# A fused attention and expert layer: maxima, values and normalising placed anew on VectorE and ScalarE

## What is computed

```python
qkv = x @ qkv_w.T + qkv_b
scores = einsum('bhtd,bhsd->bhts', q, k) * scale        # causal: -inf above the diagonal
attn = softmax(scores, axis=-1)
seq_out = einsum('bhts,bhsd->bhtd', attn, v)
...                                                     # write and read lines, decayed outer products, cumulative sums
mem_val = x @ memv_w.T + memv_b
gated = mean(sigmoid(mem_score_t * mem_scale) * gate)
y = (seq_out + gated * mem_val) @ out_w.T + out_b
x = layernorm(x + y)
x = layernorm(x + experts(x))                           # top 2 of 10, 8 real experts
```

## Time and profile before

| what | us |
|---|---|
| median of 3 runs | 800.92 |
| lowest and highest | 799.39 and 806.83 |
| the profiled execution | 804.29 |
| its span in the profile | 802.6 |

### The profile page before, as it was taken

One profiled execution on the slowest core, in us unless ns is written; L12 is line 12 of the kernel. 1 busy time (PEld: TensorE's weight loads), 2 busy tenths in 40 slices (PEclk: granted clock), 3 DMA queues, 4 the chain that ended last, 5 costly groups with the idle time before them and its releaser, 6 DMA issues.

```text
span 802.6 us, 12373 instructions
## 1 busy us (share of the span) xinstructions
PE 715.8 (89%) x4004; PEld 500.0 (62%) x4004; DVE 604.7 (75%) x2105; ACT 351.0 (44%) x701; POOL 424.7 (53%) x334
## 2 busy tenths in 40 slices
PE   5998989998989998989999986879999999999995
PEld 2555665665656666666666754457767677676774
DVE  2257776879998889788898776547777778787785
ACT  2314555555545556465554566632224232242311
POOL 9300899995675757686776860612405134051310
PEclk9997998999999999999999996879999999999998
DMA  8786462524334334334325253032030330303000
GB/s 282 253 269 214 141 190 95 191 87 142 124 97 145 130 94 147 120 107 152 95 74 167 83 172 113 1 106 80 0 106 1 105 100 7 106 1 105 27 27 26
DMA packets 60084, 89.87 MB, mean 112 GB/s; under 512 B 7898, under 2 KB 36980, under 8 KB 60020
## 3 DMA queue, kind: packets, MB, share of 16 engines
q1 hardware_dynamic: 60020, 89.09, 34.0%
HBM read 54.72 MB, written 33.82 MB: 110 GB/s over the span
## 4 chain that ended last, share of the span: by engine, by line
PE 51%; DVE 29%; ACT 6%; issue 5%; POOL 4%; DMA 4%; SPq 1%; ACTq 0%; DVEq 0%; POOLq 0%
PE ps L1252 15%; PE ps L375 9%; DVE ps L470 7%; PE ps L339 7%; PE ps L328 7%; PE ps L316 6%; DVE Ob L518 4%; DVE A L1386 3%; PE ps L232 2%; PE ps L1217 2%; ACT X L1238 2%; ACT Pr L413 2%; DVE Z L1272 1%; DVE HL L479 1%; PE ps L352 1%
## 5 line engine op out<-in xcount | busy, mean ns | idle before, releaser
L470 DVE CUSTOM_DVE_ANT_0 ps<-ps,mask 128x256 f32<-128x256 f32 (+3 forms) x512 | 237.2, 510 | 20.9 <-PE ps L316 20.3
L413 ACT ACTIVATE Pr<-ps 128x512 f32<-128x512 f32 (+2 forms) x384 | 190.0, 529 | 117.1 <-PE ps L328 111.3
L328 PE MATMUL ps<-Q,K 98*128 98x256 f32 (+2 forms) x512 | 174.0, 382 | 12.7 <-ACT Pr L413 9.1
L316 PE MATMUL ps<-K,Q 96*128 96x256 f32 (+2 forms) x512 | 153.9, 346 | 28.5 <-DVE nmax L470 28.0
L1252 PE MATMUL ps<-ew_hi,XT 128*128 128x512 f32 x512 | 176.3, 403 | 0.0
L614 POOL TENSOR_SCALAR_AFFINE_SELECT Pr<-Pr 128x512 f32<-128x512 f32 x128 | 90.3, 721 | 141.4 <-ACT Pr L413 138.9
L1386 DVE SCALAR_TENSOR_TENSOR A<-ps,cw,A 128x256 f32<-128x256 f32 x256 | 123.6, 483 | 47.2 <-PE ps L1252 34.5
L328 PEld LDWEIGHTS ps<-Q,K 98*128 98x128 f32 x512 | 93.8, 197 | 64.5 <-ACT Pr L413 27.2
L316 PEld LDWEIGHTS ps<-K,Q 96*128 96x128 f32 x512 | 100.4, 199 | 48.8 <-DVE nmax L470 36.2
L1252 PEld LDWEIGHTS ps<-ew_hi,XT 128*128 128x128 f32 x512 | 97.1, 190 | 21.3 <-issue 0.3
L1252 PE MATMUL ps<-ew_rest,XT 128*128 128x512 f32 x256 | 101.4, 396 | 0.0
(11 more groups left out here) (190 smaller groups left out, 1044.6 us busy)
## 6 DMA issues: line engine op xcount, KB each, us to landing
qk_scratch<-HL SPq DMA_DIRECT2D x32, 512.0 KB, 2.7
Q<-qk_scratch SPq DMA_DIRECT2D x96, 128.0 KB, 2.8
K<-qk_scratch SPq DMA_DIRECT2D x96, 128.0 KB, 2.7
Pr<-xT SPq DMA_DIRECT2D x8, 512.0 KB, 5.6
xraw<-xT SPq DMA_DIRECT2D x8, 512.0 KB, 4.2
mem_scratch<-Rl SPq DMA_DIRECT2D x16, 256.0 KB, 4.0
mv_scratch<-MV SPq DMA_DIRECT2D x32, 128.0 KB, 1.7
Wm<-mem_scratch SPq DMA_DIRECT2D x2, 2048.0 KB, 9.7
```

The costliest lines, as they stand in the source:

```text
L316: last = nc.tensor.matmul(o, Q[0:STACK, hh, P * i:P * i + P], K[0:STACK, hh, 0:n], start=True, stop=True)
L328: last = nc.tensor.matmul(o, K[0:STACK + 2, hh, P * kt:P * kt + P], Q[0:STACK + 2, hh, T - n:T], start=True, stop=True)
L413: nc.scalar.activation(probs(g % 2, kt, heads[0], len(heads)), src, ACT.Exp, scale=SCALE).then_inc(s_exp, 1)
L470: last = nc.vector.tensor_tensor_reduce(out=scores, in0=scores, in1=mask[:, T - w:T], scale=1.0, scalar=NEG, op0=ALU.add, op1=ALU.max, acc ...
```

## The change

- The high copy of the turned maxima goes from VectorE to ScalarE (`act_turned_max`, at unit 4 behind the exponential and the projection's copies). VectorE's subtraction goes from unit 4 to unit 5, behind its maxima and projection step.
- `dve_normalise` goes from unit 10 to unit 11, again behind both, and multiplies in one operation of four dimensions.
- `V` becomes two buffers, by batch. ScalarE writes the values straight from the projection's bank, once for each of projections 4 to 7, behind `MV`. `Vn`, `act_values`, the semaphore `s_vc` and VectorE's bias add are gone.
- The value bias goes into `bc`, which gets 512 columns; the product with `pick` runs over the whole bank. `vb` moves into a part of `Pr`, and in `fold` ScalarE and VectorE each have one operation more for `bc`.
- The weights' loads of the last batch wait for the value products of the batch before (`s_pv`) in place of `s_vc`.

```diff
-        bc = sb("bc", [STACK, D], F32R)
+        bc = sb("bc", [STACK, 2 * D], F32R)
...
-        Vn = sb("Vn", [P, QT, D], F32, part2)
+        V = [sb("V0", [P, QT, H, VW], F32, part2)]
...
+        vb = Pr[:, 1, 3456:3456 + D]
...
             if kt == 0:
-                need(pe, s_vc, 1, b, 1)
+                need(pe, s_lo, 8, b, 8)
...
-                last = nc.tensor.matmul(J_ps[:, D:2 * D], pick[:], bc[:], start=False, stop=True)
+                last = nc.tensor.matmul(J_ps[:], pick[:], bc[:], start=False, stop=True)
...
                 nc.scalar.activation(MV[:, j % 2, :], J_ps[:, D:2 * D], ACT.Identity).then_inc(s_hi, 1)
 
+                need(act, s_pv, NG, b, -NG)
+                nc.scalar.activation(V[b % 2][:, j - 4, :, 0:DH], J_ps[:, 0:D].rearrange("p (h d) -> p h d", h=H),
+                                     ACT.Identity).then_inc(s_lo, 1)
...
-        def act_values(act, b):
-            need(act, s_lo, 8, b, 8)
-            need(act, s_pv, NG, b, 0)
-            nc.scalar.activation(V[:, :, :, 0:DH], Vn[:].rearrange("p i (h d) -> p i h d", h=H),
-                                 ACT.Identity).then_inc(s_vc, 1)
+        def act_turned_max(act, b, g):
+
+            need(act, s_mtr, NG, b, g + 1)
+            if g >= 2:
+                need(act, s_mrow[g - 2], 32, b, 32)
+            else:
+                need(act, s_mrow[g + 2], 32, b, 0)
+            nc.scalar.activation(MT[:, g % 2, 0, :], M_ps[0:GROUP * QT, 0:P], ACT.Identity).then_inc(s_mt, 1)
...
-                    if g == 0 and u == 8:
-                        act_values(act, b)
+                    if u == UNITS - LEAD and not (last and g == NG - 1):
+                        act_turned_max(act, b + (g + 1) // NG, (g + 1) % NG)
...
-            else:
-                need(dve, s_vc, 1, b, 0)
-                nc.vector.tensor_tensor(Vn[:, j - 4, :], J_ps[:, 0:D], vb[:], ALU.add).then_inc(s_lo, 1)
 
         def dve_turned_max(dve, b, g):
 
-            need(dve, s_mtr, NG, b, g + 1)
-            if g >= 2:
-                need(dve, s_mrow[g - 2], 32, b, 32)
-            else:
-                need(dve, s_mrow[g + 2], 32, b, 0)
-            nc.vector.tensor_copy(MT[:, g % 2, 0, :], M_ps[0:GROUP * QT, 0:P]).then_inc(s_mt, 1)
             need(dve, s_mt, 2 * NG, b, 2 * g + 1)
...
-            for i in range(QT):
-                last = nc.vector.tensor_tensor(
-                    On[:, i, GROUP * DH * g:GROUP * DH * (g + 1)].rearrange("p (h c) -> p h c", h=GROUP),
-                    turned[:, i, :, 0:DH], rec[:, i, :].unsqueeze(2).to_broadcast([P, GROUP, DH]), ALU.mult)
-            last.then_inc(s_on, 1)
+            nc.vector.tensor_tensor(
+                On[:, :, GROUP * DH * g:GROUP * DH * (g + 1)].rearrange("p i (h c) -> p i h c", h=GROUP),
+                turned[:, :, :, 0:DH], rec[:].unsqueeze(3).to_broadcast([P, QT, GROUP, DH]),
+                ALU.mult).then_inc(s_on, 1)
...
-                    if u in (5, 11) and not last:
+                    if u in (5, 11) and g < 2 and not last:
                         dve_project(dve, b + 1, 2 * g + u // 11)
-                    if u == UNITS - LEAD and not (last and g == NG - 1):
+                    if u == UNITS - LEAD + 1 and not (last and g == NG - 1):
                         dve_turned_max(dve, b + (g + 1) // NG, (g + 1) % NG)
-                    if u == 10 and not (first and g == 0):
+                    if u == 11 and not (first and g == 0):
                         dve_normalise(dve, pb, pg)
...
                     sp.wait_ge(s_lo, NB * 8)
-                    sp.wait_ge(s_vc, NB)
+                    sp.wait_ge(s_pv, NG * (NB - 1))
...
-                nc.scalar.activation(bc[:], OT_ps[0:STACK, 0:D], ACT.Identity).then_inc(s_wr, 1)
+                nc.scalar.activation(bc[:, D:2 * D], OT_ps[0:STACK, 0:D], ACT.Identity)
+                act.wait_ge(s_ws, 5 * 16)
+                nc.scalar.activation(bc[:, 0:D], vb[0:STACK], ACT.Identity).then_inc(s_wr, 1)
...
-                nc.vector.tensor_tensor(bc[32:64], OT_ps[32:64, 0:D], bc[32:64].bitcast(F32),
+                nc.vector.tensor_tensor(bc[32:64, D:2 * D], OT_ps[32:64, 0:D], bc[32:64, D:2 * D].bitcast(F32),
+                                        ALU.subtract)
+                dve.wait_ge(s_ws, 5 * 16)
+                nc.vector.tensor_tensor(bc[32:64, 0:D], vb[32:64], bc[32:64, 0:D].bitcast(F32),
                                         ALU.subtract).then_inc(s_wl, 1)
```

More of the change, by code:

```diff
@@ L114, in build @@
         Pr = sb("Pr", [P, 2, GROUP * T * 5 // 2], F32, part2)
-        V = sb("V", [P, QT, H, VW], F32, part2)
+        V.append(sb("V1", [P, QT, H, VW], F32, part2))
         Osb = sb("Osb", [P, T], F32, part2)
@@ L181, in build @@
         s_onst = sem("s_onst")
-        s_vc = sem("s_vc")
         s_mw = [sem(f"s_mw{i}") for i in range(3)]
@@ L335, in pe_values @@
             if kt == 0:
-                need(pe, s_vc, 1, b, 1)
+                need(pe, s_lo, 8, b, 8)
                 need(pe, s_oc, NG, b, g)
             for h in range(GROUP):
-                last = nc.tensor.matmul(O_ps[32 * h:32 * h + VW, P * kt:T], V[:, kt, GROUP * g + h, :],
+                last = nc.tensor.matmul(O_ps[32 * h:32 * h + VW, P * kt:T], V[b % 2][:, kt, GROUP * g + h, :],
                                         probs(g % 2, kt, h, 1)[:, 0, :], start=(kt == 0), stop=(kt == QT - 1))
@@ L688, in build @@
             expert_w=expert_w, expert_b=expert_b, out=out, mv_scratch=mv_scratch, o_scratch=o_scratch,
-            weights_space=3 * KT * T + 2 * T + QT * D + 2 * D + 8 * KT * D + 4 + D,
+            weights_space=3 * KT * T + 2 * T + QT * H * VW + 2 * D + 8 * KT * D + 4,
             s_onst=s_onst, s_gm=s_gm, s_max=s_max, max_count=NB * PU, s_oc=s_oc, s_on=s_on, outs=NB * NG))
@@ L716, in _ @@
                              (col(SC_GB), memg_b), (col(SC_MIX), iter_mix.to_broadcast([P, 1])),
-                             (vb[:], v_b.to_broadcast([P, D]))):
+                             (vb, v_b.to_broadcast([P, D]))):
                 sp.dma_start(dst, src).then_inc(s_ws, 16)
@@ L760, in _ @@
             nc.gpsimd.memset(pick[:].bitcast(F32), 0.0).then_inc(s_cch, 1)
-            nc.gpsimd.memset(V[:, :, :, DH:VW], 1.0)
+            for v in V:
+                nc.gpsimd.memset(v[:, :, :, DH:VW], 1.0)
             nc.gpsimd.iota(iota_i[:], pattern=[[1, NE]], base=0, channel_multiplier=0)
@@ L913, in _ @@
             act.wait_ge(s_wl, 4)
+            act_turned_max(act, 0, 0)
             act_batch(act, 0, first=True)
@@ L940, in fold @@
                 nc.vector.tensor_tensor(wvc[1][:], wst_vc, wvc[0][:].bitcast(F32), ALU.subtract).then_inc(s_wl, 1)
[L941 removed]
+                nc.vector.tensor_tensor(bc[32:64, D:2 * D], OT_ps[32:64, 0:D], bc[32:64, D:2 * D].bitcast(F32),
+                                        ALU.subtract)
+                dve.wait_ge(s_ws, 5 * 16)
+                nc.vector.tensor_tensor(bc[32:64, 0:D], vb[32:64], bc[32:64, 0:D].bitcast(F32),
                                         ALU.subtract).then_inc(s_wl, 1)
             def project(j):
[L945 to L947 removed]
+                if j < 4:
+                    dve_project(dve, 0, j)
             def scores(u0):
```

4 lines of the change are left out of this document (removed).

## The result

| | us |
|---|---|
| after, median of 4 executions (791.14 to 795.53) | 792.64 |
| before, median of 3 executions (799.39 to 806.83) | 800.92 |
| ratio, with its 95% interval | 0.988 (0.985 to 0.992) |
| the profiled execution of after | 792.37 |
| its span | 790.6 |

Executions of before more than 1.5% above its fastest (811.59 beside this result, four later ones) are counted as slow and left out of every number here. The change saves about one per cent: 8.3 us between these medians, and 8.4 to 9.1 against three later medians of before (801.0, 801.6 and 801.7 over 20, 18 and 14 executions).

A forecast was written before the change was run, and what follows sets the result against it. TensorE was taken to pace groups without scans and VectorE most groups with scans, where the excess could be won. Terms summed to -5.7, with clock -1.6 to -7.3: 793.5 us from the median of 800.92, range 786 to 800.5.

The forecast's parts named there:

- opening: Before the first value products: one more ScalarE copy and VectorE subtraction for bc, less a maxima copy, +0.4; longer bias products, +0.4.
- scans at 6, 8, 10: Six groups with scans at these units: scan and maxima start sooner, normalising falls under value products; 0.8 each, -4.8 us.
- scans at 0, 2, 4: Six groups with scans at these units: VectorE saves 0.31 each, 0.34 more in three with values; -2.3 us.
- reciprocals: Four groups: a 936 ns reciprocal behind the pair at unit 4 and the normalising at unit 10 fills the wait; -2.0 us.
- rows' DMA: Copies of turned maxima, units 4 and 5: waiting for the rows' DMA was the risk; the whole term was +0.1 us.
- bias +1.7: Bias product of 512 columns for 256: 0.11 us each, 16 times on TensorE's path in eight plain groups.
- clock -1.6: Two closing waits run into half-clock stretches of 3.4 us; with shorter waits one of the two stretches goes, -1.6 us.
- last batch: Normalising behind unit 11's maxima delays the store of On and the weights' loads behind it by 0.8; +0.8 us.
- closing wait: TensorE's wait for maxima before unit 2's value products, in groups with scans at 6, 8, 10: from 1.1 to about 0.3.
- the rival in which the clock holds: All five low-clock stretches between 178 and 437 us go, 8 us instead of 1.6: about 787; chance 0.18.
- ScalarE: 0: Values and maxima copies on half-idle ScalarE delay exponentials of units 5 and 11 by 0.3 to 0.6, without cost: 0.
- The single multiply: Normalising by one multiply in place of four, which run 0.53 us: 0.2 us saved, bounds 0 to 0.3.

The follow-up runs named there:

- the two added loads: After with a spare 0.94 us VectorE reciprocal at unit 6 of twelve groups: 803.59 us in groups with scans, 793.04 us in groups without.
- before_norm_at_11: Before with only the normalising moved to unit 11, its four multiplies kept: 798.65 us.
- norm_by_group: After with the normalising at unit 11 only in groups 8, 11, 14, 17, 20 and 23, at unit 10 elsewhere: 790.12 us.
- norm_at_10: After with the normalising, still one multiply, back at unit 10: 796.62 us.
- best: After with the last batch's store of On behind the weights' loads, and normalising at unit 11 only where scans stand at 6, 8, 10: 785.43 us.
- weights_first: After with the last batch's store of On issued behind the loads of the expert stage's weights: 786.67 us.
- values_as_before: Before with the normalising and the maxima copy as changed, but values, value bias and bias product left as before: 793.79 us.
- act_copy_twice: After with ScalarE's 16x128 copy of the turned maxima made twice, first into a spare tile: 792.73 us.
- four_at_11: After with the four multiplies of before in place of the single one, still at unit 11: 794.35 us.
- copy_on_dve: After with both parts of the turned maxima back on VectorE at unit 4: 799.9 us.
- before_copy_moved: Before with only the turned maxima changed: high part copied by ScalarE at unit 4, VectorE's subtraction at unit 5: 800.17 us.

## Why the prediction was right, point by point

The total came out within 1 us of the forecast, and the claim on which all rested, that VectorE's time counts in the groups with scans and nowhere else, was shown by the two added loads. The terms behind the total were less good than their sum: errors of both signs cancelled in part, so the closeness of the total is partly luck. By stretches of the two profiled executions:

```
part                                         forecast   measured
opening, up to the first value products       +0.8       +0.35
six groups, scans at 6, 8, 10                 -4.8       -7.4
six groups, scans at 0, 2, 4                  -2.3       -3.15
reciprocals, groups 4, 5, 9 (8 is above)      -2.0       -1.75
group 3 (rows' DMA)                           +0.1       -1.9
other plain groups (bias +1.7, clock -1.6)    +0.1       +1.3
last batch                                    +0.8       +0.9
behind it                                      0         -0.3
sum                                           -7.3      -12.0
```

The 4.7 us between the two sums are partly the reference point: the profiled execution of before ran at a clock of 0.956, the mean of its 52 executions is 0.959, and the mean spans lie 9.2 apart. Point by point:

- **Scans at 6, 8, 10: -4.8, measured -7.4.** The mechanism was right and the size too small. In the four that had a clean clock on both sides (11, 14, 17, 23) a group lost 1.24 us, not 0.8. The closing wait did not fall from 1.10 to 0.3, it went. The term had counted 0.82 for the scan and the maxima that start sooner and taken a little off for unit 5 and the bias product; before_norm_at_11 shows that the move alone gives 1.2. (VectorE was busy 13.20 of the 14.71 us of group 11, just under the 90% that the prediction put it over.) Group 20 lost 2.1, with a low stretch in before; group 8 lost only 0.33 and kept a closing wait.
- **Scans at 0, 2, 4: -2.3, measured -1.25 in five of them.** The sixth, group 25, lost 1.9, and had a low stretch in before. Here the step that failed is the claim that only what VectorE is rid of counts. The normalising at unit 11 of the group ahead also stands before the scan of unit 0. It costs 2.0 us over the six, shown from both sides: before_norm_at_11 makes groups 10 and 19 0.6 slower, norm_by_group makes the six 2.0 faster, nearly all of it in groups 10, 22 and 25, which repeat in norm_at_10 and best. In the prediction it was weighed only where it stood behind scans.
- **Reciprocals: -2.0, measured -2.07** over groups 4, 5, 8 and 9. No experiment takes them alone, and groups 3 to 5 differ by up to 2 us between kernels that are alike there (group 3 takes 14.47 in after and 16.63 in weights_first); the agreement is not a proof. That norm_at_10, norm_by_group and best are slower in groups 4 and 5 than every other kernel made from after speaks for the term.
- **Bias product: 0.22 a plain group, measured 0.24.** values_as_before has no such growth. In the opening TensorE's wait for `bc` grew from 0.44 to 1.07, 0.63 for the 0.7 of the sum; the first value products came 0.35 later than in before, where +0.8 was forecast. VectorE's first maxima copy, gone from there, is the 0.3 that was priced: TensorE's wait for the first maxima went from 1.98 to 1.67.
- **Last batch: +0.8, measured +0.87** over groups 28 to 31. VectorE's wait for the weights grew by 0.57 (6.25 to 6.82), and the store starts 9.67 us after the value products of group 28 instead of 9.03. But 0.87 is less than the clock can move here: groups 29 to 31 of act_copy_twice, with the same placement, are 2.1 shorter than those of after.
- **Rows' DMA: +0.1.** TensorE's waits for the rows were 3.4 us in total in before and 2.4 in after: no cost. The 1.9 won in group 3 are mostly this wait, 2.51 and 1.36, and the rest goes with a low stretch (a clock of 0.90 in before, 1.00 in after); the wait is 1.95 in best and not an effect that holds.
- **ScalarE: 0.** Its waits went from 9.1 to 11.3 us, and a further copy in each group changed nothing. The 16x128 copy took 0.25, where 0.28 was taken; the Trainium skill (ScalarE: Activation LUTs, What ACT_TABLE_LOAD costs) gives 293 ns by estimate, a little more than the trace.
- **The single multiply** took 425 ns for 620: 0.2 saved, as priced. four_at_11 is 1.7 us slower, but not in the groups at 6, 8, 10, where it was to count; 0.2 each shows in groups 16, 18 and 19, and the rest lies where the clock is low in one of the two. Its worth is under 2 us and not settled closer. The estimate from the Trainium skill (VectorE: DVE Perf Modes, the section on the TRN2 errata) of 0.47 saved is not what the rows show.
- **The clock: -1.6, measured about -2.7.** The low stretches between 174 and 448 us went from five to one in the profiled executions. The prediction counted on one fewer and named a change of more than one as a sign that it was wrong; by that sign this term was wrong. Over all executions the mean clock rose by 0.0044, which goes with 2.7 us. So the rival in which the clock holds came true in the profiled execution, and over all executions for a third of its 8 us, which is why the total did not come near its 787.

So two gains were taken too small, the closing waits (by 0.4 in each of four groups) and the clock (by 1.1), and against them stood a give-back that was not seen (2.0 in the groups at 0, 2, 4). Set against mean spans the forecast of -7.3 was 2 short; set against the median of three it was given from, 1 short.

## What to carry to other kernels

Where one engine alternates between being early and being late, place a movable piece of its work by group, not once for the whole loop: behind the urgent work where it is late at the end, ahead of its wait where it is late at the next beginning. The same move saved 1.2 us in each group of one kind and cost up to 0.9 in those of the other. When a change moves the time by about a per cent, compare groups of equal kind in the traces and the mean clock of all executions before an edit is credited with the total: a copy seemed worth 7.3 us in one kernel and 1.5 in the other, and by the line through the spans more than half of the difference was clock.

## What was not expected of the hardware

The clock falls in whole pieces: each low stretch lasted 3.4 us at the 1.2 GHz level, or a multiple. Waits of TensorE of 1.2 to 1.8 us were followed by one in some kernels and not in others, at the same place of the work: 1.78 us at 236.67 and full clock in after, 1.78 at 238.20 and a clock of 0.57 behind it in copy_on_dve; best has waits of 1.77 and 1.78 at the same places and no low clock between 174 and 448 us. The Trainium skill (TensorE: Matmul & The Clock Gate, What's actually happening) ties the clock to activity. The traces agree in that each stretch in the attention before the last batch stands at or behind a wait, but they do not say which wait is followed, and a short one can be: in act_copy_twice the clock falls in group 17 (14.64 us instead of 13.35) behind waits of 0.29 and 0.41 us. A low stretch costs nearly its full 1.7 us where TensorE sets the pace: group 6 takes 14.47 with one in best, 12.85 without in norm_by_group. In group 24 of before it cost nothing: 14.07 us with a clock of 0.88, and 14.02 at full clock in before_copy_moved, where TensorE waited 1.45 us for maxima instead. One program fell into two bands, clocks of 0.966 and 0.956, some six microseconds apart, which is most of the spread that a median of three or four executions has to deal with here.
